# GroupNorm, 1x1 ternary convolution and residual on one core: seven instead of five chunks kept in SBUF between the two passes, a load ring of five instead of seven, mean and squares of a chunk in turn, and the last store in two parts

## What is computed

```python
def _act_quant(x):
    xc = jnp.clip(x, -8.0, 8.0)
    s = jnp.maximum(jnp.max(jnp.abs(xc)), EPS) / 127.0      # one number for all of x
    return jnp.clip(jnp.round(xc / s), -127, 127) * s
def _gn(v, G=32, eps=1e-5):
    g = v.reshape(B, G, C // G, H, W)
    m = jnp.mean(g, axis=(2, 3, 4), keepdims=True)
    s = jnp.var(g, axis=(2, 3, 4), keepdims=True)
    return ((g - m) / jnp.sqrt(s + eps)).reshape(v.shape)
out = x + conv1x1(_act_quant(_gn(x)), ternary(weight))
```

## Time and profile before

| | |
|---|---|
| median of 3 runs | 1868.37 us |
| profiled execution | 1868.27 us |
| its span (first to last instruction) | 1866.5 us |
| moved by DMA | 526.42 MB read from HBM, 268.44 MB written |
| mean over the span | 426 GB/s |
| busy share of PE, DVE, ACT, POOL | 57%, 72%, 58%, 24% |
| pass 1 | up to about 640 us |
| scale known, first activation of pass 2 | 656.77 us |
| first store issued | 662.59 us |

### The profile page before, as it was taken

The page is one execution under the profiler, slowest core; times in us unless marked ns, Lnnn a source line. Parts: engine busy times, 40 slices in busy tenths (PEclk is TensorE's granted clock), DMA queues, the critical chain, the costliest instruction groups (busy, mean ns, idle before and its releaser), DMA issues.

```text
span 1866.5 us, 10231 instructions
## 1 busy us (share of the span) xinstructions
PE 1061.7 (57%) x2239; PEld 313.8 (17%) x2239; DVE 1336.5 (72%) x711; ACT 1086.7 (58%) x797; POOL 451.9 (24%) x380
## 2 busy tenths in 40 slices
PE   0999999999999646533333433334333433344332
PEld 0333333333333211100000000000000000000000
DVE  4999999999999979846555665566555665566553
ACT  0999999999999757634444444434443444434441
POOL 0777777777777400000000000000000000000000
PEclk9999999999999855555555555555555555555555
DMA  9999999999999999999999999999999999999998
GB/s 407 429 427 428 428 429 429 428 428 428 429 428 428 428 351 429 430 431 431 431 431 431 432 431 431 430 432 431 431 431 431 431 431 431 430 432 431 431 431 368
DMA packets 55035, 795.00 MB, mean 426 GB/s; under 512 B 6256, under 2 KB 6256, under 8 KB 6256
## 3 DMA queue, kind: packets, MB, share of 16 engines
q1 hardware_dynamic: 36144, 526.40, 66.3%
q10 hardware_dynamic: 18880, 268.48, 33.6%
HBM read 526.42 MB, written 268.44 MB: 426 GB/s over the span
## 4 chain that ended last, share of the span: by engine, by line
DMA 65%; DVE 16%; ACT 6%; issue 4%; POOL 2%; another core or an unknown queue 2%; PE 2%; SPq 0%; ACTq 0%; DVEq 0%; POOLq 0%
DMA out_dram<-ring 36%; DMA ring<-in_x_dram 29%; DVE square_maxs L486 7%; DVE ring L594 6%; ACT ring L319 3%; POOL levels L295 2%; ACT levels L422 2%; PE product L637 1%; DVE levels L588 1%; DVE first_sq_maxs L496 1%; ACT levels L401 0%; ACT product L312 0%; PE product L633 0%; ACT product L336 0%
## 5 line engine op out<-in xcount | busy, mean ns | idle before, releaser
L674 PE MATMUL product<-levels,w_lhsT 128*128 128x512 bf16 x1024 | 483.3, 627 | 705.6 <-DVE levels L588 705.6
L422 ACT ACTIVATE levels<-ring,tile_affine 128x2048 int16<-128x2048 f32 x240 | 490.8, 2090 | 582.7 <-DMA ring<-in_x_dram 568.5
L594 DVE SCALAR_TENSOR_TENSOR ring<-product,out_scale,ring 128x2048 f32<-128x2048 f32 (+1 forms) x258 | 600.8, 2329 | 0.1
L486 DVE TENSOR_REDUCE square_maxs<-ring 128x4096 f32 (+1 forms) x119 | 522.8, 4416 | 34.7 <-ACT ring L319 34.6
L588 DVE TENSOR_SCALAR levels<-levels 128x2048 bf16<-128x2048 int16 (+1 forms) x258 | 176.6, 684 | 445.0 <-ACT levels L422 434.3
L295 POOL TENSOR_TENSOR levels<-ring 128x512 f32<-128x512 f32 x360 | 449.5, 1278 | 182.2 <-DMA ring<-in_x_dram 179.7
L319 ACT ACTIVATE ring<-ring,group_stats 128x4096 f32<-128x4096 f32 x119 | 440.4, 3701 | 0.0
L637 PE MATMUL product<-levels,neg_mean 128*128 128x512 f32 x720 | 364.8, 617 | 12.6
L674 PEld LDWEIGHTS product<-levels,w_lhsT 128*128 128x128 bf16 x1024 | 110.2, 130 | 1078.2 <-DVE levels L588 823.5
L633 PE MATMUL product<-ring,neg_mean 128*128 128x512 f32 x480 | 236.5, 615 | 3.1 <-DMA ring<-in_x_dram 2.1
L637 PEld LDWEIGHTS product<-levels,neg_mean 128*128 128x128 f32 x720 | 118.4, 189 | 240.2 <-POOL levels L295 206.8
(11 more groups left out here) (82 smaller groups left out, 56.2 us busy)
## 6 DMA issues: line engine op xcount, KB each, us to landing
ring<-in_x_dram SPq DMA_DIRECT2D x251, 2048.0 KB, 15.2
out_dram<-ring ACTq DMA_DIRECT2D x126, 2048.0 KB, 44.7
out_dram<-ring ACTq DMA_DIRECT2D x4, 1024.0 KB, 5.6
levels<-in_L_conv_weight_dram ACTq DMA_DIRECT2D x2, 16.0 KB, 8.4
```

Source lines behind the costliest of these rows:

```text
L422: nc.scalar.activation(levels[:, h, :], halves[:, 2 * s + h, :], ACT.Identity, bias=tile_affine[:, a, 1, :], scale=tile_affine[:, a, 0, :] ...
L486: nc.vector.tensor_reduce(square_maxs[:, bass.ds(k + 1, 1)], ring[:, slot1(REST + g), :], AX_X, ALU.max).then_inc(maxed, 1)
L594: nc.vector.scalar_tensor_tensor(part, product[:, h, at], out_scale[:, :], part, ALU.mult, ALU.add).then_inc(combined, 1)
L674: mm = pe.matmul(product[:, h, n * BANK:(n + 1) * BANK], w_lhsT[:, :], ints[:, h, n * BANK:(n + 1) * BANK], start=True, stop=True)
```

## The change

Seven chunks of image 0 are kept and the ring has five slots; there are twelve slots as before. `TURN` is 10 and `PRE` 10, so the loop has 11 turns. The squares of the seven kept chunks are made in 14 pieces of 2048 columns: four after the ring chunks 2, 4, 6 and 8, one in each of the ten turns of the loop. ACT runs `close(g)` right ahead of `squares(g)`. The statistics in the middle of the last turn become smaller: only what the scale and image 0 need is made there; the reciprocal roots of all other groups, and the matmul that picks each row's own statistics, move into pass 2, behind chunk 3 of image 0. In pass 2 the first store comes behind the first activation of chunk 1, and that activation waits for two matmul groups instead of three. The last chunk is stored by two DMAs, of 120 rows and of 8 rows.

```diff
-KEPT = 5
-RING1 = 7
+KEPT = 7
+RING1 = 5
-TURN = 2 * RING1
-PRE = 8
+TURN = 10
+PRE = 10
+PIECE = 2048
+FIRST_PIECES = [2, 4, 6, 8]
...
+    MOST = P - P // 16
...
             def squares_of_kept(j):
+                if not (isinstance(j, int) and j == 0):
+                    act.wait_ge(kept_maxed, j)
...
-            close(0, 0)
             for g in range(PRE):
-                close(g + 1, 0)
+                close(g, 0)
                 squares(g, 0)
-                if g == 1:
-                    squares_of_kept(0)
+                if g in FIRST_PIECES:
+                    squares_of_kept(FIRST_PIECES.index(g))
             with act.Fori(0, TURNS - 1) as t:
                 for g in range(PRE, PRE + TURN):
-                    close(g + 1, t)
+                    close(g, t)
                     squares(g, t)
...
-                if g == PRE + 4:
-                    roots(1, 0, SOON)
+                if g == PRE + 3:
+                    variances(1, 0, SOON)
+                    act.wait_ge(var_kept, 1)
+                    nc.scalar.activation(std[:, 0:1], var_eps[:, 0:1], ACT.Sqrt).then_inc(std_guess, 1)
...
-            store_half(0, 0)
             for c in range(1, TC):
...
-                    act.wait_ge(multiplied, EXTRA + (2 * c + h - 1))
+                    act.wait_ge(multiplied, 2 if c == 1 and h == 0 else EXTRA + (2 * c + h - 1))
                     nc.scalar.activation(levels[:, h, :], halves[:, 2 * s + h, :], ACT.Identity,
                                          bias=act_affine[:, 1, 0:1], scale=act_affine[:, 0, 0:1]).then_inc(scaled, 1)
-                    if c == 1:
-                        store_half(h, 1 - h)
-                    elif c == 2 and h == 0:
-                        store_half(1, 1)
-                if c > 2:
+                    if c <= HALVED:
+                        store_half(c - 1, h)
+                if c > HALVED:
                     store(0, c - 1)
+                if c == 2:
+                    act.wait_ge(var_kept, 2)
+                    nc.scalar.activation(std[:, 1:N1 + 1], var_eps[:, 1:N1 + 1], ACT.Sqrt).then_inc(std_guess, 1)
...
-            store(TILES - 1, TC - 1)
+            s = slot2(2, TC - 1)
+            act.wait_ge(combined, EXTRA + TILES * 2 * TC)
+            for rows in (slice(0, MOST), slice(MOST, P)):
+                act.dma_start(out_rows[TILES - 1, TC - 1][rows, :], ring[rows, s, :]).then_inc(stored[s], 16)
...
+            def largest_of(n, first, cols):
+                at = slice(first, first + cols)
+                dve.wait_ge(var_kept, n)
+                then(nc.vector.reciprocal(recip_var[:, at], var_eps[:, at]))
+                then(nc.vector.tensor_tensor(square_maxs[:, at], square_maxs[:, at], recip_var[:, at], ALU.mult))
+                then(nc.vector.tensor_reduce(largest_so_far[:, n - 1:n], square_maxs[:, at], AX_X, ALU.max))
...
-                elif g == PRE + 6:
-                    statistics(1, 0, SOON)
-                    largest_of(0, 0, SOON)
+                if g == PRE + 3:
+                    largest_of(1, 0, SOON)
+                    reciprocal_roots(1, 0, 1)
...
             def affine_of_rest():
+                reciprocal_roots(2, 1, N1)
+                dve.wait_ge(picked, 1)
...
+                        if isinstance(t, int) and t == 0 and c == 4 and h == 0:
+                            pe.wait_ge(combined, u)
+                            pe.wait_ge(stats_ready, 2)
+                            pe.matmul(picked_ps, pick[:, :], group_stats[:, :, 1:N1 + 1],
+                                      start=True, stop=True).then_inc(picked, 1)
```

More of the change, by code:

```diff
@@ L130, in preact_quant_conv_kernel @@
         parity = small(2)
-        taken[0] = FOLD
-        var_eps = small(N1 + 1)
-        std = small(N1 + 1)
-        work = small(2 * (N1 + 1)).rearrange("p (s n) -> p s n", s=2)
         product = ctx.enter_context(nc.psum_tensor("product", [P, 2, HALF], F32))
@@ L257, in _ @@
                 last = max(m for m in range(KEPT, CHUNKS) if slot2(m // TC, m % TC) == s)
[L258 removed]
+                sp.wait_ge(stored[s], 16 * uses2(last // TC, last % TC) + (16 if last == CHUNKS - 1 else 0))
         @block.gpsimd
@@ L338, in squares_of_kept, with variances @@
                                      accum_out=first_sq_sums[:, bass.ds(j + REST, 1)]).then_inc(kept_squared, 1)
-            def roots(n, first, cols):
+            def variances(n, first, cols):
                 act.wait_ge(var_made, n)
-                nc.scalar.activation(std[:, first:first + cols], var_ps[:, first:first + cols], ACT.Sqrt,
-                                     scale=-1.0, bias=eps[:, :]).then_inc(std_guess, 1)
+                nc.scalar.activation(var_eps[:, first:first + cols], var_ps[:, first:first + cols], ACT.Identity,
+                                     scale=-1.0, bias=eps[:, :]).then_inc(var_kept, 1)
             act.wait_ge(filled, 7)
@@ L466, in _ @@
                                     ALU.mult).then_inc(w_tern_ready, 1)
+            then(nc.vector.tensor_scalar(w_small[:, 4:5], w_small[:, 1:2], 0.5 / QMAX, None, ALU.mult))
             dve.wait_ge(w_transposed, 1)
@@ L495, in maxima_of_kept @@
                 dve.wait_ge(kept_squared, j + 1)
-                return nc.vector.tensor_reduce(first_sq_maxs[:, bass.ds(j + REST, 1)], kept_squares, AX_X, ALU.max)
-            half_rstd = group_stats[:, 1, :]
-            rstd_square = work[:, 1, :]
-            def statistics(n, first, cols):
+                nc.vector.tensor_reduce(first_sq_maxs[:, bass.ds(j + REST, 1)], kept_squares, AX_X,
+                                        ALU.max).then_inc(kept_maxed, 1)
+            double_rstd = group_stats[:, 1, :]
@@ L512, in statistics @@
                 dve.wait_ge(stats_ready, n)
-            def largest_of(n, first, cols):
-                at = slice(first, first + cols)
-                then(nc.vector.tensor_tensor(work[:, 0, at], square_maxs[:, at], rstd_square[:, at], ALU.mult))
-                then(nc.vector.tensor_reduce(largest_so_far[:, n:n + 1], work[:, 0, at], AX_X, ALU.max))
             for i in range(REST):
@@ L575, in _ @@
                                     ALU.mult).then_inc(quant_ready, 1)
-            then(nc.vector.tensor_scalar(out_scale[:, :], amax[:, 4:5], 1.0 / QMAX, w_small[:, 1:2],
+            then(nc.vector.tensor_scalar(out_scale[:, :], amax[:, 0:1], amax[:, 5:6], w_small[:, 4:5],
                                          ALU.mult, ALU.mult))
+            own = own_chunk[:, :].rearrange("p (t k) -> p t k", t=1).broadcast_to([P, TILES - 1, TC])
             def affine_of_rest():
+                reciprocal_roots(2, 1, N1)
+                dve.wait_ge(picked, 1)
+                for i in range(2):
+                    at = picked_ps[:, i * N1:(i + 1) * N1].rearrange("p (t k) -> p t k", k=TC)
+                    then(nc.vector.tensor_tensor(by_row[:, i, :, :], at, own, ALU.mult))
                 then(nc.vector.tensor_reduce(row_stats[:, :, 1:TILES], by_row[:, :, :, :], AX_X, ALU.add))
-                then(nc.vector.tensor_scalar(act_affine[:, 0, 1:TILES], row_stats[:, 1, 1:TILES], amax[:, 5:6], 2.0 * QMAX,
-                                             ALU.mult, ALU.mult))
+                then(nc.vector.tensor_scalar(act_affine[:, 0, 1:TILES], row_stats[:, 1, 1:TILES], amax[:, 5:6],
+                                             0.25 * QMAX, ALU.mult, ALU.mult))
                 nc.vector.tensor_tensor(act_affine[:, 1, 1:TILES], act_affine[:, 0, 1:TILES], row_stats[:, 0, 1:TILES],
@@ L658, in _ @@
             pe.matmul(var_ps[:, N1:N1 + 1], neg_mean1[:, :], tail_sum[:, :], start=False, stop=True).then_inc(var_made, 1)
-            pe.wait_ge(stats_ready, 2)
-            pe.matmul(picked_ps, pick[:, :], group_stats[:, :, :].rearrange("p s n -> p (s n)"),
-                      start=True, stop=True).then_inc(picked, 1)
             pe.wait_ge(rows_maxed, 1)
```

84 lines of the change are left out of this document (38 added, 46 removed).

## The result

The changed kernel takes **1878.96 us** (median of five executions, 1875.81 to 1880.99), the kernel before, run beside it, 1868.34: 10.6 us more, a ratio of 1.0056 with a 95% interval of 1.0043 to 1.0068. A sixth execution, in the slow state (1954.37 us, granted clock 0.602 instead of 0.674), is left out of these figures. Forecast was 1853.5 in a range of 1850 to 1861, and faster. The profiled execution took 1878.96 us, its span 1877.2.

A forecast was written before the change was run, and what follows sets the result against it. The prediction took the DMA engines to bound the kernel. Its terms -9.7 + 0 + 2.6 - 4.0 - 3.7 = -14.8 us, on the profiled 1868.27, gave 1853.5 us, range 1850 to 1861.

The forecast's parts named there:

- In the steady state I take 0: Pass 1, ring of five: loads have room enough, so 0 us; upper end 6 us, ten turns losing 0.6 each.
- rival (b): Pass 1 pays more through kept pieces, start and statistics: up to 1863.6 us; chance 0.12.
- 1.1 us or more: Pass 1: spare time of a ring load, 10.6 us from issue to landing against loads of 9.0 and 9.5.
- rival (d): Five-slot ring starves in pass 1 if loads keep needing 12.7 us: +45 us, 1898; chance 0.07.
- The start, +2.6: Start of the ring: four close early pieces make DVE free slots late, +2.6 us, ends 0 and 5.3.
- They shrink to 1.4 to 4.2 us; I take 2.2: Statistics on DVE in the middle of the last turn: three wide and three narrow operations, 2.2 us taken.
- Two loads less, -9.7: Two more chunks of image 0 aren't read a second time: -9.7 us, if DMA engines don't stand still longer.
- -4.0: Between the passes: DMA engines lose 4.7 us instead of 8.7, so -4.0 us; ends -2.6 and -7.2.
- Rival (c): Saved loads fall where DMA engines stand still anyway, and the first store comes no sooner: 1867.2 us; chance 0.04.
- The scale comes earlier: End of pass 1: first quarter of pass 2 at 648.4 us instead of 656.77, 651.0 with the late start.
- The last store, -3.7: End of pass 2: splitting into 120 and 8 rows leaves out the late DMA engine, -3.7 us.
- Rival (a): Last store: the late engine isn't the one left out, 1857.2 to 1857.8 us; chance 0.22.

The follow-up runs named there:

- e5: e1 with each kept piece cut to its first 8 of 2048 columns, every wait and instruction staying: 1857.29 us.
- e6: e1 with 28 kept pieces of 1024 columns, eight early after ring chunks 2 to 9 and two in each turn: 1863.95 us.
- e10: e1 with 28 kept pieces of 1024 columns, one after ring chunk 16 and three in each of nine turns: 1859.19 us.
- e3: e1 with five kept chunks and a ring of seven again, the rest of the change staying: 1859.31 us.
- e4: e1 with six kept chunks and a ring of six, twelve pieces of 2048 columns: 1857.71 us.
- e1: The changed kernel with the last chunk stored by one DMA of 128 rows: 1875.22 us.
- e7: e3 with close(g + 1) ahead of squares(g) again, as in the kernel before: 1860.34 us.

## Why the prediction was wrong, point by point

Forecast was -14.8 us, measured +10.6: 25.4 us apart.

- **"In the steady state I take 0"**, upper end 6 for ten turns of 0.6 us: **11.6 us**. The mechanism is the one of the upper end and of rival (b); the size failed. The delay was right: behind the piece of each turn the issue came 6.5 us after the one before, 1.6 us late (forecast: 1.7). The room, "1.1 us or more", was not. A load in the even flow takes 10.0 us (e5), not 10.6, since 14.5 us pass from landing to the next issue and not 13.9. The loads behind the ten pieces took 8.2 to 10.3 us, 9.1 in the mean, near the 9.0 and 9.5 of the earlier trace rows; that is a room of 0.9 us in the mean and of none in the turn shown above. And in half of the turns the load after the late one was late as well, which the formula leaves out. A delay of 0.8 us (a piece of 1024 columns) was borne, one of 1.6 not. A ring has to bear the largest single delay. e5, e6 and e10 tell this from a ring that is too short in itself, rival (d): with tiny, or with small and even pieces the ring holds. The sign named for (d), landing times over 11 us, didn't come; the rate fell to 418 GB/s at a median of 9.9.
- **The start, +2.6**, ends 0 and 5.3: **3.8 us** (5.1, less 1.3 that before has too), inside the ends.
- **"They shrink to 1.4 to 4.2 us; I take 2.2"**: the statistics took 631.75 to 636.34, **4.6 us**, in the timeline of DVE:

```profile
631.75 0.84 DVE L517 RECIPROCAL recip_var<-var_eps 128x111 f32<-128x111 f32 x1
632.62 1.34 DVE L518 TENSOR_TENSOR square_maxs<-square_maxs,recip_var 128x111 f32<-128x111 f32 x1
634.30 0.16 DVE L525 RECIPROCAL var_eps<-square_sums 128x1 f32<-128x1 f32 x1
634.50 0.62 DVE L526 TENSOR_TENSOR group_stats<-square_sums,recip_var 128x1 f32<-128x1 f32 x1
635.15 1.19 DVE L527 TENSOR_TENSOR group_stats<-group_stats,var_eps 128x1 f32<-128x1 f32 x1
```

  A one-column product took up to 1.19 us; width wasn't what set the price, and the narrow steps should have been bounded by L507's 1.21 like the wide ones. The 0.22 of the earlier trace rows was read at 653.72 us, when POOL had no more to do; here POOL was folding:

```profile
633.79 1.31 POOL L299 TENSOR_TENSOR levels<-ring 128x512 f32<-128x512 f32 x1
635.05 1.27 POOL L299 TENSOR_TENSOR levels<-ring 128x512 f32<-128x512 f32 x1
```

  L526 ends at 635.12 and L527 at 636.34, each 0.02 us after the POOL addition beside it. The statistics delayed slots as a kept piece does, and the last chunk by 1.5 us, which the forecast had no term for.
- **"Two loads less, -9.7"**: 2.0 us net in e5 against e3, 0.1 in e10, and 1.6 for the first of them alone (e4). The bytes are saved, but "as long as the DMA engines don't stand still longer for it" was waved through: I counted the gaps between the passes with seven and with five loads, found them shorter in the end, and gave -4.0 on top. e3 shows that the earlier scale alone fills the stretch (429, 430, 427); taking loads out opens it again: 3.5 us between the passes, 1.9 at the last chunk, and 1.6 by an end that is 18.3 us in e3 and 19.9 in e5, which leaves -2.7 of the -9.7 (the two spans differ by 2.1). Rival (c), "the two loads saved are those of the stretch in which the DMA engines stand still anyway", was nearer for this term; its other half, that the first store comes no sooner, is refuted by every kernel without late loads (654.6 to 658.7 instead of 662.6).
- **The scale comes earlier**: right. "Without the slip 648.4" for the first quarters; e3 has 648.74, e4 649.41. In the changed kernel the chain is 8.0 us shorter from folding to store, the forecast's 7.4 with the slip taken out. Halves 2.9 us apart: 3.1.
- **"The last store, -3.7"**: **+3.7** in the changed kernel (5.0 by the ends of the two profiled executions, after and e1), +3.75 in the kernel before. Rival (a) gave at most +0.6. The late engine wasn't the point: that the split itself could slow its packets was not considered, though no row of before showed a store of fewer than 128 rows, so the cost had to be bounded from above as well. The rule that I weighed, in the Trainium skill's page "DMA: Bandwidth & Descriptors", section "Why a DMA increments its semaphore by 16 and not by 1", tells how many engines a row count uses and nothing of how fast they then are.

Together: 11.6 + 1.2 + 1.5 + 7.4 (from -3.7 to +3.7) = 21.7 of the 25.4. The other 3.7 are of the size of what the two saved loads failed to bring (e5 stands 1857.3 against the forecast's 1853.5 + 3.7 - 2.6 = 1854.6). I can't place it better, since in the changed kernel the late loads and the gap between the passes overlap.

A version that beats both kernels is e4: six kept, ring of six, a whole last store and everything else of the change.

## What to carry to other kernels

A shorter ring is judged by its longest single delay against the room of one load, and not by the mean rates of its engines alone; side work that must pass through the same engines goes in small, even pieces. A transfer saved pays only where the DMA engines would have been busy: look at what else would fill the stretch it is taken from. A store is better split by columns than by rows, if at all.

## What the chip showed unexpectedly

- Two stores of 120 + 8, 112 + 16 or 64 + 64 rows in place of one of 128 cost 2.9 to 3.75 us at the end of a kernel, two of 128 rows and half the columns 0.4, which can't be told from nothing.
- A single DMA engine is late at the end of the kernel before, e1 and e4, by seven to nine packets of 0.6 us; in e3, e5 and e10 it is alone for one to four. Why stays open. The Trainium skill's page "DMA: Bandwidth & Descriptors", section "Latency and other measured facts", ties slow engines to copies issued from GpSimd; this kernel issues all its large ones from SP and ACT, and one is late all the same.
- A product of one column took 0.16 to 1.19 us on DVE, depending on when it ran: 1.19 and 0.62 at 635 us while POOL folds chunks, 0.16 at 666 us when POOL is idle. The traces show the wait: among the statistics near the end of pass 1, in the kernel before, the changed one, e1, e3 to e7 and e10, every DVE product of two SBUF tensors that began while a POOL addition ran ended 0.01 to 0.13 us after that addition did, whether of 1 or of 107 columns. The three of 107 or 111 columns that began between two additions took 0.27 us, and reciprocals, which read one tensor, were not held (0.16 us for one column beside POOL).
